# Writing 768 finished rows one by one from SyncE and ScalarE instead of by GpSimd's scatters

## The reference

```
edge_feat = concat([x[rcv], x[snd], attr, weight])          # per edge
score     = silu(silu(edge_feat @ W1 + b1) @ W2 + b2) @ W3 + b3
alpha     = softmax of score over the edges of one receiver
out       = segment_sum(x[snd] @ Wv * alpha * node_weight[snd], rcv)
result    = layernorm(x + (x + out))                        # per node
```

## Time and profile before

| | us |
|---|---|
| median of 3 runs | 998.13 |
| lowest and highest run | 997.67, 998.24 |
| span of the profiled execution, first to last instruction | 996.1 |
| POOL busy | 752.3 (76% of the span) |
| PE busy | 575.9 |
| DVE busy | 573.2 |
| ACT busy | 522.6 |

### The profile page before, as it was taken

How to read it: one execution, slowest core, us unless ns; L and a number is a source line. 1 busy time by engine, 2 the same in 40 slices (tenths; PEclk the granted TensorE clock), 3 DMA queues, 4 the chain that set the end, 5 groups by cost and what they waited for, 6 DMA issues and landing times.

```text
span 996.1 us, 10941 instructions
## 1 busy us (share of the span) xinstructions
PE 575.9 (58%) x2587; PEld 394.8 (40%) x2587; DVE 573.2 (58%) x2275; ACT 522.6 (52%) x1168; POOL 752.3 (76%) x790
## 2 busy tenths in 40 slices
PE   0989999988704457677667666777996600000000
PEld 0656766665502223455445444545675500000000
DVE  6987887773452737597698987953678841000000
ACT  0356655554523756777698979974786630000000
POOL 6777777777777777777777777777777777777777
PEclk9999999999998776788788988878999855555555
DMA  7799999989965877788778878763452231111111
GB/s 208 227 302 315 321 320 333 336 233 311 330 226 161 288 256 245 273 292 268 273 272 283 292 234 317 246 185 91 129 124 79 71 78 53 53 51 52 53 53 45
DMA packets 85079, 206.12 MB, mean 207 GB/s; under 512 B 19797, under 2 KB 56566, under 8 KB 72472
## 3 DMA queue, kind: packets, MB, share of 16 engines
q1 hardware_dynamic: 56728, 140.95, 41.7%
q0 software_dynamic: 28288, 64.48, 22.8%
HBM read 113.16 MB, written 92.31 MB: 206 GB/s over the span
## 4 chain that ended last, share of the span: by engine, by line
POOL 38%; issue 23%; PE 20%; ACT 13%; DVE 5%; DMA 0%; POOLq 0%; ACTq 0%; DVEq 0%
POOL hk L422 23%; POOL out_rows L426 15%; ACT xin L478 6%; PE bank L622 5%; PE bank L638 4%; PE bank L645 3%; PE bank L624 2%; ACT hk L530 2%; PE bank L616 2%; PE bank L609 2%; ACT hkT L501 1%; ACT x L511 1%; ACT zs L521 1%; PE bank L597 1%; DVE dst L899 1%
## 5 line engine op out<-in xcount | busy, mean ns | idle before, releaser
L478 ACT ACTIVATE xin<-xin,drs 128x128 f32<-128x128 f32 x637 | 258.1, 484 | 51.6 <-DVE drs L884 51.5
L422 POOL DMA_INDIRECT hk<-in_xw,snd_t x196 | 188.0, 959 | 62.0 <-issue 59.4
L426 POOL DMA_INDIRECT out_rows<-hk,sidx_t x196 | 188.8, 963 | 59.7 <-issue 59.4
L422 POOL DMA_INDIRECT region<-rec_d,id_t x196 | 186.8, 953 | 59.7 <-issue 59.1
L422 POOL DMA_INDIRECT hk<-in_x,kg_t x196 | 186.6, 952 | 59.7 <-issue 59.7
L899 DVE BATCH_NORM_STATS2 dst<-xin 128x6 f32<-128x256 f32 x392 | 137.0, 414 | 61.6 <-DMA xin<-in_x 61.0
L577 PE MATMUL bank<-w1b,region 128*128 128x128 f32 x392 | 149.1, 484 | 13.8 <-ACT region L488 7.8
L622 PE MATMUL bank<-hkT,w1a 128*128 128x512 f32 x98 | 73.2, 839 | 138.8 <-issue 98.3
L577 PEld LDWEIGHTS bank<-w1b,region 128*128 128x128 f32 x392 | 99.8, 315 | 33.9 <-ACT region L488 10.1
L622 PEld LDWEIGHTS bank<-hkT,w1a 128*128 128x128 f32 x98 | 20.1, 240 | 175.5 <-issue 163.2
L511 ACT ACTIVATE x<-bank,bcol 128x512 f32<-128x512 f32 x49 | 33.5, 683 | 95.0 <-PE bank L624 95.0
(11 more groups left out here) (176 smaller groups left out, 853.0 us busy)
## 6 DMA issues: line engine op xcount, KB each, us to landing
xin<-in_x SPq DMA_DIRECT2D x49, 1024.0 KB, 8.2
out_rows<-xin SPq DMA_DIRECT2D x49, 1024.0 KB, 5.2
rec_d<-hk SPq DMA_DIRECT2D x49, 514.0 KB, 7.7
krow<-seg_d SPq DMA_DIRECT2D x49, 128.0 KB, 3.5
hk<-in_xw,snd_t POOLq DMA_INDIRECT x196, 5.8
hk<-in_x,kg_t POOLq DMA_INDIRECT x196, 3.9
region<-rec_d,id_t POOLq DMA_INDIRECT x196, 3.6
out_rows<-hk,sidx_t POOLq DMA_INDIRECT x196, 2.2
```

Of the source, the lines that this page charges most:

```text
L422: pool.indirect_dma_start(out=to, out_offset=None, in_=frm, in_offset=bass.IndirectOffsetOnAxis(ap=index, axis=0)).then_inc(done, 16)
L426: pool.indirect_dma_start(out=out, out_offset=bass.IndirectOffsetOnAxis(ap=index, axis=0), in_=frm, in_offset=None).then_inc(done, 16)
L478: ins = nc.scalar.activation(xin[:, j % X_RING, n, :], xin[:, j % X_RING, n, :], ACT.Identity, bias=drs[:, j % 2, 1, n:n + 1], scale=drs[: ...
```

## The change

Of the 196 tiles of finished rows the first six (`ROW_TILES`, 768 rows, groups 0 and half of group 1) are no longer scattered by POOL. Each of their rows is written by a DMA of its own, from one partition of `hk` to the row of `out` whose number stands in a register. SP writes the first 480 rows, ScalarE the other 288. For this

- SP writes the six columns of `sidx_t` to HBM (`list_d`) once, behind `tab_ready`, right before the second part.
- `store_rows` is a generator. For every 32 rows it loads 32 numbers from `list_d` into registers of the issuing engine, and then issues one DMA at each `next`.
- SP waits, behind `dense_written`, for the list and for `res_ready` of group 0. It issues 6 rows at the end of each later step (38 to 66), and the rest behind the loads for the repair.
- ScalarE begins after its last step: 64 rows ahead of the repair's exponential, 32 between it and the repair's scalings, and the rest behind them.
- POOL's scatters start at the third tile of group 1; its waits and SP's last ones count the tiles that are left. SP also waits for all the rows.

```diff
+ROW_TILES, SP_ROWS = 6, 480
+ALL_ROWS = ROW_TILES * P
+LIST_READ, TAIL_ROWS, ACT_BEFORE, ACT_BETWEEN = 32, 6, 64, 32
...
+    list_d = nc.dram_tensor("list_d", (1, ALL_ROWS), I32).ap()
...
+        def tiles_scattered(g):
+            return [q for q in range(TPG) if g * TPG + q >= ROW_TILES]
+
+        def wait_scattered(eng, r, to):
+            n = sum(len(tiles_scattered(g)) for g in range(r, to, SC_SEMS))
+            if n > 0:
+                eng.wait_ge(scattered[r], 16 * n)
+
+        def store_rows(eng, kind, first, last, done):
+            for o in range(first, last, LIST_READ):
+                _, rows = nc.values_load_multi_w_load_instructions(
+                    list_d[0:1, o:o + LIST_READ], [kind], min_val=0, max_val=NOUT - 1,
+                    skip_runtime_bounds_check_because="the sorted keys and the numbers of the spare rows are rows of out")
+                for n, r in enumerate(rows, o):
+                    t, p = n // P, n % P
+                    eng.dma_start(out[bass.ds(r, 1), :], hk[p:p + 1, t // TPG, t % TPG, :]).then_inc(S[done], 16)
+                    yield
...
+            sp.wait_ge(S["tab_ready"], 1)
+            sp.dma_start(list_d.rearrange("o (t p) -> p (o t)", p=P), sidx_t[:, 0:ROW_TILES],
+                         allow_slow_non_contiguous=True).then_inc(S["list_out"], 16)
...
+            finished = store_rows(sp, mybir.EngineType.SP, 0, SP_ROWS, "sp_rows")
 
             for s in range(LAST_STEP):
...
                     sp.sem_inc(S["dense_written"], 1)
+                    sp.wait_ge(S["list_out"], 16)
+                    sp.wait_ge(S["res_ready"], (SP_ROWS - 1) // GE + 1)
+                elif B0 + s > DSTEP[-1] + 3:
+                    for _ in range(TAIL_ROWS):
+                        next(finished, None)
...
+            for _ in finished:
+                pass
             for r in range(SC_SEMS):
-                sp.wait_ge(scattered[r], 16 * TPG * len(range(r, G, SC_SEMS)))
+                wait_scattered(sp, r, G)
+            sp.wait_ge(S["sp_rows"], 16 * SP_ROWS)
+            sp.wait_ge(S["act_rows"], 16 * (ALL_ROWS - SP_ROWS))
             sp.wait_ge(S["fix_out"], 32)
...
-                    wait_ring(pool, scattered, g - SC_SEMS, 16 * TPG)
-                    for q in range(TPG):
+                    wait_scattered(pool, g % SC_SEMS, g - SC_SEMS + 1)
+                    for q in tiles_scattered(g):
...
+            finished = store_rows(act, mybir.EngineType.Activation, SP_ROWS, ALL_ROWS, "act_rows")
+            act.wait_ge(S["dense_written"], 1)
+            act.wait_ge(S["list_out"], 16)
+            act.wait_ge(S["res_ready"], (ALL_ROWS - 1) // GE + 1)
+            for _ in range(ACT_BEFORE):
+                next(finished)
             act.wait_ge(S["fexp_ready"], 1)
             nc.scalar.activation(fe, fe, ACT.Exp).then_inc(S["fexp_done"], 1)
+            for _ in range(ACT_BETWEEN):
+                next(finished)
             act.wait_ge(S["chain_f"], STEPS)
...
             ins.then_inc(S["fix_res"], 1)
+            for _ in finished:
+                pass
```

More of the change, by code:

```diff
@@ L245, in gnn_kernel @@
             "parts_ready", "parts_out", "fix_ready", "fixT_done", "fexp_ready", "fexp_done", "fixY_ready", "fixY_done",
-            "fix_stats", "chain_f", "fix_res", "fix_out")}
+            "fix_stats", "chain_f", "fix_res", "fix_out", "list_out", "sp_rows", "act_rows")}
         hs_in = [sem(f"hs_in{r}") for r in range(HS_RING)]
```

## The result

The changed kernel takes 1003.33 us as the median of 4 runs (1002.79 to 1004.82), beside 997.90 us for the kernel before on the same chip. The ratio is 1.0056, with a 95% interval of 1.0041 to 1.007. It is slower by 0.56%: the second rival, not the forecast.

The account below looks back on a forecast made before the run. The prediction took POOL's number of instructions to bound the kernel: 996.1 - 7.6 + 0 (SP) + 0 (ACT) + 0 (repair) = 988.5 us of span, with 2.0 us more for the median 990.5 us; range 989.5 to 1030.

Parts of the forecast that it names:

- the second rival: SyncE's rows behind the repair's loads end the kernel: 805.5 + 372c us at c us a row; chance 0.24.
- What bounds the kernel, and what is taken away: The number of POOL's instructions sets the end; six tiles not scattered, at 1.268 us each, save 7.6 us.
- rival 4: Loads of keys come late near group 36 and POOL's last gathers wait; needs about 14 us of lag; chance 0.02.
- Price of one row: On the issuing engine, 0.25 + 0.04 + 0.07 + 0.07 = 0.43 us a row, within 0.25 to 1.2 us.
- SyncE's formula: SP's last row at 800.8 + 372c us; 960.8 us at c = 0.43 us a row, 25 us before the deadline.
- Price of a loaded register: In the list load, the skill's about 200 ns for each register from HBM, giving an estimated 0.56 us a row.
- The limit: Price of a row on SyncE up to which its rows stay hidden behind POOL: 0.50 us.
- the hidden case: All added work on SyncE and ScalarE hides behind POOL: 990.5 us, own range 989.5 to 993; chance 0.62.
- ScalarE's rows: After its steps, 288 rows end at 931.3 us, limit 0.62 us a row; chance 0.08 that they end the kernel.
- Lock between the issuers: SP and ACT issuing together from 806 us might wait for each other: 0.68 us for 306 rows, 1042 us.
- Repair, list, DMA load: Repair's loads 15 to 20 us later, writing the list once, and 768 more packets: no cost to the end.
- Rival 5: At POOL's scatters or the closing, waits or a slower pace eat the 7.6 us; time stays 998 us; chance 0.04.

Follow-up runs that it names:

- e2: Changed kernel with 16 row numbers to each list load instead of 32; 1010.62 us, one run.
- e6: Changed kernel with 384 rows on SyncE instead of 480, so 384 on each engine; 1011.97 us, one run.
- e1: Changed kernel with 32 rows moved from SyncE to ScalarE (448 and 320); 989.62 us, ratio 0.9921 to the kernel before.
- e7: Changed kernel with 512 rows on SyncE instead of 480 and 256 on ScalarE; 1019.55 us, one run.

## Why the prediction was wrong

*What bounds the kernel, and what is taken away*: this was right. A scatter takes 1.269 us and POOL ends 7.0 us earlier. Every version that covers its rows is at 989.6 to 991.1 us, around the forecast of 990.5. What is missing of the 7.6 us is mostly the first scatter, 0.4 us late. The sign that I gave for rival 4 did show, a gather near 738 us behind TensorE, but with 1.5 us in total and not as what sets the end.

*Price of one row*: this is the step that failed. I took 0.43 us, and wrote that it was the weakest number; 0.526 us was measured. The DMA was nearly as priced: 224 ns beside 221 and 253, of which my sum had 0.25 us. I had one gap of 0.04 us for a row, but three instructions carry three gaps, 0.118 us together. So it is 0.408 us from row to row without the list, where my sum has 0.36. And the list load was one trip of 2.2 us in my sum, 0.07 us a row; it is 3.78 us, 0.118 us a row, and goes by the number of registers (e2). Each of the two is 0.05 us, and over 372 rows they make 36 us, against the 25 us by which SP's last row was to come ahead of its deadline.

*SyncE's formula*: its form was right. 805.5 + 372 x 0.526 = 1001.2 us, measured 1003.3; the 2.1 us are the rest of larger errors. SP's last row is issued 5 us later than 800.8 + 372 x 0.526 = 996.5, as the last steps end later (787.78 instead of 782.65 us for the last load of keys). The span ends 1.5 us behind it instead of 2.7, and the median of the runs lies 0.3 us above the profiled span instead of 2.0, as the profiled execution was the slowest of the four. The burst at "the dearest of all" was also summed wrongly: with rows of 0.62 us it is 21.3 and not 19.8 us. Nothing hangs on it.

*Price of a loaded register*: the Trainium skill ("Runtime: NRT & Kernel Launch", section Instruction fetch mechanics) has about 200 ns for a register loaded from HBM. The runs disagree in the figure, 118 ns, and agree in its form: by the register, bulk or not. The estimate by it, 0.56 us, was nearer to 0.526 than mine and on the right side of the limit of 0.50.

*The limit*: I had the limit at 0.50 us and a range for the price of 0.25 to 1.2 us. With the limit in the lower third of the range, 0.62 for the hidden case leant on one untested number.

*ScalarE's rows*: the price was sized too low here too, 0.48 to 0.50 us each instead of 0.43, but it stays below ScalarE's limit of 0.62 and the rows were covered. The rest of the formula was short: 807.5 + 288 x 0.483 = 946.6 us, while ScalarE ended at 959.6 us. Its last normalization ended at 810.67 instead of 805.77 us, with waits of 0.7 and 1.7 us for stores of y, for which I had seen more room. And it waited 5.7 us ahead of the exponential (841.32 to 847.03 us), since the repair's loads were not 15 to 20 but 31.4 us late (826.51 instead of 795.08). e6 shows that this side can end the kernel too.

*Lock between the issuers*: the Trainium skill ("Perfetto Trace Analysis", section DMA Instruction — HWDGE) has the descriptor generator locked for exclusive use. In the changed kernel no issue of SP is longer beside ScalarE (224 ns in the median, 268 ns at most) than it can be alone (224 and up to 295 ns), and e1, e6 and e7 come out without such a term.

*Repair, list, DMA load*: there was no cost at the end of the kernel, as forecast; the exponential moved from 816.18 to 847.03 us and nobody waited for the repaired rows. *Rival 5*: it is excluded by e1.

## What to carry to other kernels

Work that is moved off the bounding engine is a gain only as far as the engines that take it still end before the bounding one. Write down the limit of the unit price first, and where an untested price lies near it, give the new work less than the sum allows: here 32 rows of 768 were the difference between 0.56% slower and 0.79% faster. Price a register-addressed DMA by all its sequencer instructions and their gaps, and a load of registers by the number of registers; sequencer time is in no busy share and, as here, may be absent from the chain.

## What the runs showed of the hardware

- A load of registers from HBM takes 3.78 us for 32 and 1.96 us for 16, from SBUF 2.23 us for 32. Even from SBUF it is 0.07 us for each register.
- A DMA of one 512-byte row with an address in a register is issued in 224 ns on SP and 213 ns on ACT, about as long as a y store (221 and 253 ns); with its arithmetic the rows follow at 0.41 us on SP.
- A DMA of one row with a fixed address in a scratch tensor, without register instructions between, spread from 215 to 554 ns on SP, 253 in the median. Whether it is the closeness of the issues or the other target that makes them longer stays open.
- SP's issues stayed at 224 ns while ScalarE issued rows of its own every 0.39 us, (12.17 - 0.21) / 31 in its 32 rows from 850.86 us on.
